# Records of the edges scattered straight from their tiles, 224 in the dense layers' block and 168 behind the experts' stores

## The chip, the cores and the metric

The kernel runs on one core of a Trainium2 chip. A core has the engines PE (TensorE, matrix products), VectorE (DVE), ScalarE (ACT), GpSimd (POOL) and SyncE (SP), which here only issues DMAs. Each engine runs its own stream of instructions, in order, and they meet at semaphores. The metric is device time in microseconds of one execution, the median of several runs.

## What is computed

A graph of 3125 nodes with 256 channels and 50000 edges (src, dst), sorted by dst, passes two layers, each a graph part and a feed-forward part, with a layer norm ahead of each part and a residual sum behind it:

```python
edge_index = jnp.stack([src, dst])
x = x + _L0_gnn_ref(_layernorm(x), edge_index, ...)   # sum of x[src] at dst, then 256-512-1024-512-256 with batch norm and elu
x = x + _L0_ffn_ref(_layernorm(x)[None], ...)[0]      # 8 experts, top 2 of a router, silu(x w1) * (x w3), then w2
x = x + _L1_gnn_ref(_layernorm(x), ..., edge_index)   # attention over edges: e = exp(leaky(el[src] + er[dst])), sums at src
x = x + _L1_ffn_ref(_layernorm(x)[None], ...)[0]      # the half of the nodes with the largest weights goes through gelu(x w1) w2
```

The second graph part sums at src, while the edges come sorted by dst. So the kernel sorts them anew, by the block of 125 nodes that src lies in, and this sorting is what the change touches.

## The kernel before

The program is a row of blocks. At the end of each block all engines meet at a barrier. In order, with the times of the profiled execution:

- 0 to 546 us, edges of the first layer: GpSimd gathers 128 rows at a time of the normalised x (L312, 392 indirect DMAs), PE sums them by one-hot matrices, VectorE adds the sums. Beside it VectorE ranks each edge within its source block.
- 546 to 1065 us, the dense layers (four matmul layers with batch norm). VectorE first turns the ranks into places, tile `posd` (L714, ready at 587.9 us). Then GpSimd scatters the records.
- 1065 to 1224 us, the router of the experts: layer norm, logits, top 2, places of the rows in tiles of 128 by expert; GpSimd scatters the normalised rows to `xs_d` (L976, 50 indirect DMAs), and the experts' weights are split in two f16 halves.
- 1224 to 1624 us, the experts: 56 tiles of 128 rows, in one block with the router. For each tile PE makes `psH` and `psY`, ScalarE writes `yv`, and GpSimd stores `yv` to `y_d` (L983).
- 1624 to 1720 us the results are gathered and added and the table of the second graph part is written; 1720 to 2326 us the edges of the second layer; 2326 us to the end its feed-forward part.

A record is 8 bytes for an edge: its place in its source block and its dst. Tile `rec` (128 partitions x 392 columns x 2) holds them, tile `posd` (128 x 392) the place of each in the DRAM tensor `rec_d`. Both lie untouched in SBUF until the second layer's edges, where `rec_d` is loaded. One indirect DMA scatters one column, 128 records, so 392 of them are needed (T1 = 392). They are made in 49 rounds (R1) of 8 columns, each round in two halves of four (HT = 4). `stage` (L590 to L600) makes a half: two copies on GpSimd bring the four columns of `posd` to `stp` (L592) and of `rec` to `str_` (L593), a wait on `s_stg` lets them finish, and four indirect DMAs (L597) read the small tiles. Since the small tiles have two halves, each half waits on `s_sc[h]` until the scatters of the half before it in the same place have landed.

LATE = 12 sets where they stand. In the dense layers' block GpSimd makes the first 37 rounds, 296 scatters: two halves in straight code, then a hardware loop (L627). The other 12 rounds, 96 scatters, stand in the experts' block, in a loop in which each store of a tile is followed by one half (L985); in a second loop the other 32 stores follow without scatters (L990). At the end of the block GpSimd waits until all scatters and stores have landed. GpSimd does nothing else in the dense block but one memset. All of this is written in program order; no scheduler moves it.

SyncE loads in the dense block, behind the third layer's matmuls, x again (`x2`), the bias `b4` and the raw weights of four of the eight experts (L565, L570), those of the others at the start of the router's block.

Of the kernel before, what the change touches and what calls it, by code (L numbers as in the profile page):

```python
# [31 lines left out]
I32 = mybir.dt.int32  # L32
# [12 lines left out]
TPR = 8  # L45
HT = TPR // 2
R1 = -(-E // (ET * TPR))
T1 = R1 * TPR
# [10 lines left out]
T2 = (K2 * N + X * 127) // 128  # L59
# [16 lines left out]
def wait_apart(eng, sem, value, tick):  # L76


    eng.wait_ge(sem, value)
    eng.sem_inc(tick, 1)  # L80


def loop(nc, eng, start, end):

    return nc.Fori(start, end, engines=[eng.engine], hint_back_edge=True)
# [25 lines left out]
def program(nc, a, out):  # L111
    with ExitStack() as ctx:
        taken = []

        def sem(name):
            taken.append(nc.alloc_semaphore(name))
            return taken[-1]
# [10 lines left out]
        KB = 1024  # L128
        BASE = 16512

        def at(name, offset, shape, dt=F32):
            return nc.alloc_sbuf_tensor_at(name, shape, dt, offset=BASE + offset)

        def dram(name, shape, dt=F32):
            return nc.dram_tensor(name, shape, dt, kind="Internal").ap()

        xn_d = dram("xn_d", (N, D))
        rec_d = dram("rec_d", (ET, T3 * 2), I32)
# [4 lines left out]
        rec = at("rec", 1 * KB, [128, T1, 2], I32)  # L143
# [94 lines left out]
        s_halves = sem("s_halves")  # L238
# [277 lines left out]
        behind = at("behind", 101 * KB, [T3 // HT, HT, NB])  # L516
        blk_i = at("blk_i", 101 * KB + 512, [T3 // HT, HT], I32)
        posd = at("posd", 1 * KB + 3136, [128, T1], I32)
        stp = at("stp", 1 * KB + 4704, [128, 2, HT], I32)
        str_ = at("str_", 1 * KB + 4736, [128, 2, HT, 2], I32)  # L520
        LATE = 12
        blk_d = dram("blk_d", (1, T3), I32)
        zero = at("zero", 153 * KB, [128, D])
        xs_d = dram("xs_d", (T2 * 128, D))
# [6 lines left out]
        s_pos = sem("s_pos")  # L531
        s_blk = sem("s_blk")
        s_blkst = sem("s_blkst")
        s_stg = sem("s_stg")
        s_sc = [sem("s_sc0"), sem("s_sc1")]
        s_sq = sem("s_sq")
        s_sd = sem("s_sd")
# [41 lines left out]
        with ExitStack() as p2:  # L579
# [7 lines left out]
                f = ZIN[l][:, k, :].bitcast(F16)  # L587
                return f[:, bass.ds(c0 * 2, w)], f[:, bass.ds(c0 * 2 + w, w)]

            def stage(pool, g, h):  # L590

                nc.gpsimd.tensor_copy(stp[:, h, :], posd[:, bass.ds(g * TPR + h * HT, HT)])  # L592
                nc.gpsimd.tensor_copy(str_[:, h, :, :], rec[:, bass.ds(g * TPR + h * HT, HT), :]).then_inc(s_stg, 1)  # L593
                pool.wait_ge(s_stg, g * 2 + h + 1)
                pool.sem_inc(s_halves, 1)
                for j in range(HT):
                    pool.indirect_dma_start(  # L597
                        out=rec_d.rearrange("p (t r) -> (p t) r", r=2),
                        out_offset=bass.IndirectOffsetOnAxis(ap=stp[:, h, j:j + 1], axis=0),
                        in_=str_[:, h, j, :], in_offset=None).then_inc(s_sc[h], 16)  # L600

            @block.sync
            def _(sp):
# [14 lines left out]
            @block.gpsimd  # L618
            def _(pool):
                ch = Chain(pool, s_c2[0])  # L620
                nc.gpsimd.memset(zero[:, :], 0.0).then_inc(s_zero, 1)

                pool.wait_ge(s_recst, 16)
                pool.wait_ge(s_pos, 1)
                stage(pool, 0, 0)
                stage(pool, 0, 1)
                with loop(nc, pool, 1, R1 - LATE) as g:  # L627
                    for h in range(2):
                        pool.wait_ge(s_sc[h], g * (16 * HT))
                        stage(pool, g, h)  # L630

            def rows_of(l, m):

# [258 lines left out]
        yv = at("yv", o, [128, 2, D]); o += 2048  # L892
        y_d = dram("y_d", (T2 * 128, D))
# [29 lines left out]
        s_yv = sem("s_yv")  # L923
        s_yst = [sem("s_yst0"), sem("s_yst1")]

        with ExitStack() as p3:
# [36 lines left out]
            @block.gpsimd  # L963
            def _(pool):
                ch = Chain(pool, s_c3[0])
                nc.gpsimd.memset(ones3[:, :], 1.0)
                ch.step(nc.gpsimd.memset(later3[:, :], 1.0))
                ch.step(nc.gpsimd.affine_select(out=later3[:, :], in_=later3[:, :], compare_op=ALU.is_gt, fill=0.0,
                                                base=0, pattern=[[1, PB]], channel_multiplier=-1))
                pool.sem_inc(s_k3, 1)  # L970

                pool.wait_ge(s_slot, 1)
                for b in range(NB):
                    for k in range(K2):
                        j = b * K2 + k
                        pool.indirect_dma_start(  # L976
                            out=xs_d, out_offset=bass.IndirectOffsetOnAxis(ap=slot_i[:, j:j + 1], axis=0),
                            in_=xn2[:, b, :], in_offset=None).then_inc(s_scx, 16)


                def store(t, i):
                    wait_apart(pool, s_yv, 1 + t + 1, s_halves)
                    pool.dma_start(y_d[bass.ds(t * 128, 128), :], yv[:, i, :]).then_inc(s_yst[i], 16)  # L983

                with loop(nc, pool, 0, LATE) as g:  # L985
                    for i in range(2):
                        store(g * 2 + i, i)
                        pool.wait_ge(s_sc[i], (g + (R1 - LATE)) * (16 * HT))
                        stage(pool, g + (R1 - LATE), i)
                with loop(nc, pool, LATE, T2 // 2) as g:  # L990
                    for i in range(2):
                        store(g * 2 + i, i)
                for h in range(2):
                    pool.wait_ge(s_sc[h], 16 * HT * R1)
                for i in range(2):
                    pool.wait_ge(s_yst[i], 16 * (T2 // 2))

# [930 lines left out]
```

## Time and profile before

| | us |
|---|---|
| three runs | 2622.04, 2623.48 (median), 2626.05 |
| the profiled execution, its own time | 2622.28 |
| its span | 2620.7 |
| GpSimd busy | 1480.6 (56%) |
| PE busy | 1861.2 (71%) |
| VectorE busy | 1496.4 (57%) |
| ScalarE busy | 631.6 (24%) |

The profile gives for each engine the times at which it executed. "Idle before" an instruction is time in which the engine had nothing running, with the releaser that ended it; "issue" is time in which it waited for nothing that the profile shows, and a releaser such as PEq L579 is the sequencer of another engine at a barrier. Since blocks are closed by barriers, the engine that ends a block last sets its length, and idle time of the others there costs nothing.

### The profile page before, as it was taken

The page shows a single profiled execution, that of the slowest core. Times are in us where ns is not written, and L with a number is a line of the kernel's source. Part 1 is how long each engine was busy: PE and PEld are TensorE (multiplying, and loading weights), DVE is VectorE, ACT ScalarE, POOL GpSimd, SP SyncE. Part 2 cuts the span into 40 slices and gives each one's busy share as a digit, 9 for nine tenths or more (in the row PEclk, how much of TensorE's full clock was granted, in tenths as well). Part 3 has the DMA queues.
Part 4 walks back from the last instruction along what each step waited for, and adds up shares of the span by engine and source line. Part 5 has one row for each costly group of instructions (what it writes and reads, how often), then busy time and mean ns, then how long its engine had stood idle before and what let it go on. Part 6 is the DMA issues. An engine that isn't in the chain of part 4 may idle for free. (4 is left out here: it accounts for less than half of the span.)

```text
span 2620.7 us, 37949 instructions
## 1 busy us (share of the span) xinstructions
PE 1861.2 (71%) x9564; PEld 1336.1 (51%) x9565; DVE 1496.4 (57%) x3214; ACT 631.6 (24%) x1252; POOL 1480.6 (56%) x1583
## 2 busy tenths in 40 slices
PE   3988889898979650405999996267788777731597
PEld 2766667743434340403666664256566656620366
DVE  7666544465567370471333333646666666668698
ACT  4000000025566340151333332121111111110343
POOL 3777777717777777174662002757777777751000
PEclk8555665588989875557999998568887888865699
DMA  7333333340000230321111111321111111120100
GB/s 219 106 102 104 104 105 104 105 139 1 1 1 1 74 113 1 128 72 55 37 37 37 39 36 41 89 59 25 26 25 25 25 25 25 25 12 0 25 24 26
DMA packets 112944, 144.01 MB, mean 55 GB/s; under 512 B 46660, under 2 KB 82372, under 8 KB 112764
## 3 DMA queue, kind: packets, MB, share of 16 engines
q0 software_dynamic: 60160, 86.81, 13.8%
q1 hardware_dynamic: 52729, 56.58, 7.0%
q8 instruction: 20, 0.33, 0.0%
q14 instruction: 35, 0.29, 0.0%
HBM read 114.00 MB, written 29.18 MB: 55 GB/s over the span
## 5 line engine op out<-in xcount | busy, mean ns | idle before, releaser
L1484 POOL DMA_INDIRECT g<-tab_d,recs x416 | 460.0, 1106 | 148.8 <-issue 126.5
L597 POOL DMA_INDIRECT rec_d<-str__1722,stp x392 | 393.2, 1003 | 172.5 <-issue 94.6
L497 PE MATMUL psA<-oh,G 128*128 128x128 f32 x1568 | 433.4, 438 | 73.6 <-DMA G<-xn_d,gat_i 35.7
L312 POOL DMA_INDIRECT G<-xn_d,gat_i x392 | 378.6, 966 | 145.0 <-issue 134.3
L497 PEld LDWEIGHTS psA<-oh,G 128*128 128x128 f32 x1568 | 340.4, 303 | 166.6 <-issue 93.2
L1625 PE MATMUL psS<-vv,oh 128*125 128x260 f32 x832 | 307.9, 523 | 128.6 <-DVE acc L1560 128.6
L1625 PEld LDWEIGHTS psS<-vv,oh 128*125 128x125 f32 x832 | 180.4, 245 | 222.1 <-DVE acc L1560 183.1
L825 PE MATMUL psZ<-z,W 128*128 (+1 forms) x1344 | 264.0, 359 | 27.0 <-DVE z L739 27.0
L447 DVE TENSOR_TENSOR accT<-accT,psA 128x256 f32 x392 | 165.0, 421 | 167.6 <-PE psA L497 141.6
L643 ACT ACTIVATE z<-psZ,vec 128x500 f32 (+2 forms) x112 | 70.8, 633 | 640.7 <-PE psZ L818 530.9
L1234 PE MATMUL psH<-we,xh 128*128 x1344 | 214.7, 310 | 0.5 <-issue 0.5
L825 PEld LDWEIGHTS psZ<-z,W 128*128 128x128 f16 x1344 | 124.5, 98 | 166.4 <-issue 39.3
L1560 DVE TENSOR_TENSOR acc<-acc,psS 125x260 f32 x416 | 176.6, 424 | 43.6 <-PE psS L1625 2.4
L983 POOL DMA_DIRECT2D y_d<-yv x56 | 31.3, 558 | 237.6 <-ACT yv L1041 236.9
L1234 PEld LDWEIGHTS psH<-we,xh 128*128 128x128 f16 x1344 | 130.6, 98 | 60.6 <-issue 8.1
L1493 ACT ACTIVATE ohT<-psOT 125x512 f32<-125x512 f32 x104 | 62.1, 597 | 379.6 <-PE psOT L1609 379.6
L1549 DVE TENSOR_TENSOR vv<-g,pp 128x1040 f32<-128x1040 f32 x104 | 128.6, 1236 | 23.1 <-PE psS L1625 17.0
L1617 PEld LDWEIGHTS psE<-el,ohT 125*128 125x128 f32 x832 | 130.5, 224 | 13.2 <-issue 2.4
L1150 DVE SCALAR_TENSOR_TENSOR hv<-psH,sl 128x384 f32<-128x384 f32 x112 | 57.5, 513 | 129.6 <-ACT sl L1029 129.6
L1144 DVE SCALAR_TENSOR_TENSOR xh<-psTx,xh 128x256 f16<-128x256 f32 x56 | 23.8, 424 | 182.8 <-ACT xh L1023 182.8
L1255 PE MATMUL psY<-we,hh 128*128 (+1 forms) x1008 | 125.3, 273 | 1.1 <-DVE hh L1157 1.1
L1617 PE MATMUL psE<-el,ohT 125*128 x832 | 116.1, 263 | 1.8 <-ACT ohT L1493 1.8
(253 smaller groups left out, 2728.4 us busy)
## 6 DMA issues: line engine op xcount, KB each, us to landing
raw<-in_L_ffn_w SPq DMA_DIRECT2D x16, 682.0 KB, 9.3
xs_d<-zero SPq DMA_DIRECT2D x1, 7168.0 KB, 23.9
xs<-xs_d SPq DMA_DIRECT2D x56, 128.0 KB, 2.0
y_d<-yv POOLq DMA_DIRECT2D x56, 128.0 KB, 2.0
g<-tab_d,recs POOLq DMA_INDIRECT x416, 2.5
G<-xn_d,gat_i POOLq DMA_INDIRECT x392, 2.7
rec_d<-str__1722,stp POOLq DMA_INDIRECT x392
raw<-in_L_ffn_w SPq DMA_DIRECT2D x16, 384.0 KB, 9.8
```

Source lines behind the costliest of these rows:

```text
L312: pool.indirect_dma_start(out=G[:, i, :], out_offset=None, in_=xn_d, in_offset=bass.IndirectOffsetOnAxis(ap=gat_i[:, t:t + 1], axis=0)).th ...
L447: nc.vector.tensor_tensor(accT[:, :, bass.ds(at_[i], WIN)], accT[:, :, bass.ds(at_[i], WIN)], psA[i // 2][:, i % 2, :, :], ALU.add).then_i ...
L497: last = nc.tensor.matmul(psA[i // 2][:, i % 2, h, :], G[:, i, 128 * h:128 * (h + 1)], oh[:, i, :], start=True, stop=True)
L597: pool.indirect_dma_start(out=rec_d.rearrange("p (t r) -> (p t) r", r=2), out_offset=bass.IndirectOffsetOnAxis(ap=stp[:, h, j:j + 1], axis=0),
L825: last = nc.tensor.matmul(psZ[m % 4][:, 0:w], W[l][:, sw, k, ms], halves(l, k, c * CW, w)[sh], start=(n == 0), stop=(n == len(terms) - 1))
L1234: last = nc.tensor.matmul(psH[2 * w3 + q][:, 0:HC[q]], xh[:, i, sx, 128 * k:128 * (k + 1)], weights(e, 2 * w3 + k, sw, q * HQ, HC[q]), sta ...
L1255: last = nc.tensor.matmul(psY[:, :], hh[0:KP[m], i, sh, 128 * m:128 * (m + 1)], weights(e, 4 + n, sw, (m - 3 * n) * D, D)[0:KP[m], :], sta ...
L1484: pool.indirect_dma_start(out=g3[:, n % BODY, j, :], out_offset=None, in_=tab_d, in_offset=bass.IndirectOffsetOnAxis(ap=recs[:, t, 1:2], a ...
L1549: nc.vector.tensor_tensor(vv[:, s % 2, :, :].rearrange("p j (h f) -> p j h f", h=NH), g3[:, s, :, NH:RW].unsqueeze(2).to_broadcast([128, H ...
L1560: nc.vector.tensor_tensor(b, b, psS[j][:, :], ALU.add).then_inc(s_ac, 1)
L1617: last = nc.tensor.matmul(psE[s % 2][:, j, :], ohT[:, s % 2, 128 * j:128 * (j + 1)], el[:, bass.ds(at_[j] * NH, NH)], start=True, stop=True)
L1625: last = nc.tensor.matmul(psS[j][:, :], oh3[:, s, j, :], vv[:, s % 2, j, :], start=True, stop=True)
```

## The change

The staging is taken out. `record(pool, t)` issues one indirect DMA that reads its 128 places from column t of `posd` and its records from column t of `rec`; the tiles `stp` and `str_`, the semaphore `s_stg` and the waits for landed halves go. The split between the blocks is now by columns: EDGES_EARLY = 224 in the dense layers' block, and behind each of the 56 stores of the experts PER_TILE = 3, 168 in all. Both are straight code in place of hardware loops, and the store addresses are constants. The waits at the end of the experts' block remain.

```diff
-        stp = at("stp", 1 * KB + 4704, [128, 2, HT], I32)
-        str_ = at("str_", 1 * KB + 4736, [128, 2, HT, 2], I32)
-        LATE = 12
+        EDGES_EARLY = 224
+        PER_TILE = (T1 - EDGES_EARLY) // T2
+        assert EDGES_EARLY + PER_TILE * T2 == T1
...
-            def stage(pool, g, h):
-
-                nc.gpsimd.tensor_copy(stp[:, h, :], posd[:, bass.ds(g * TPR + h * HT, HT)])
-                nc.gpsimd.tensor_copy(str_[:, h, :, :], rec[:, bass.ds(g * TPR + h * HT, HT), :]).then_inc(s_stg, 1)
-                pool.wait_ge(s_stg, g * 2 + h + 1)
-                pool.sem_inc(s_halves, 1)
-                for j in range(HT):
-                    pool.indirect_dma_start(
-                        out=rec_d.rearrange("p (t r) -> (p t) r", r=2),
-                        out_offset=bass.IndirectOffsetOnAxis(ap=stp[:, h, j:j + 1], axis=0),
-                        in_=str_[:, h, j, :], in_offset=None).then_inc(s_sc[h], 16)
+            def record(pool, t):
+                pool.indirect_dma_start(
+                    out=rec_d.rearrange("p (t r) -> (p t) r", r=2),
+                    out_offset=bass.IndirectOffsetOnAxis(ap=posd[:, t:t + 1], axis=0),
+                    in_=rec[:, t, :], in_offset=None).then_inc(s_sc[t % 2], 16)
...
                 pool.wait_ge(s_recst, 16)
                 pool.wait_ge(s_pos, 1)
-                stage(pool, 0, 0)
-                stage(pool, 0, 1)
-                with loop(nc, pool, 1, R1 - LATE) as g:
-                    for h in range(2):
-                        pool.wait_ge(s_sc[h], g * (16 * HT))
-                        stage(pool, g, h)
+                for t in range(EDGES_EARLY):
+                    record(pool, t)
...
                 def store(t, i):
-                    wait_apart(pool, s_yv, 1 + t + 1, s_halves)
-                    pool.dma_start(y_d[bass.ds(t * 128, 128), :], yv[:, i, :]).then_inc(s_yst[i], 16)
-
-                with loop(nc, pool, 0, LATE) as g:
-                    for i in range(2):
-                        store(g * 2 + i, i)
-                        pool.wait_ge(s_sc[i], (g + (R1 - LATE)) * (16 * HT))
-                        stage(pool, g + (R1 - LATE), i)
-                with loop(nc, pool, LATE, T2 // 2) as g:
-                    for i in range(2):
-                        store(g * 2 + i, i)
-                for h in range(2):
-                    pool.wait_ge(s_sc[h], 16 * HT * R1)
+                    pool.wait_ge(s_yv, 1 + t + 1)
+                    pool.dma_start(y_d[t * 128:(t + 1) * 128, :], yv[:, i, :]).then_inc(s_yst[i], 16)
+
+                for t in range(T2):
+                    store(t, t % 2)
+                    for j in range(PER_TILE):
+                        record(pool, EDGES_EARLY + t * PER_TILE + j)
+                for i in range(2):
+                    pool.wait_ge(s_sc[i], 16 * (T1 // 2))
                 for i in range(2):
                     pool.wait_ge(s_yst[i], 16 * (T2 // 2))
```

What stands in a row on GpSimd in the dense layers' block before; the copies fill the small tiles, each DMA row is four scatters, and the second part is the body of a hardware loop of 36 rounds:

```order
L621 MEMSET zero 128x256
L592 COPY stp<-posd 128x4
L593 COPY str__1722<-rec 128x8
L597 DMA rec_d<-str__1722,stp 53248x2 x4
L592 COPY stp<-posd 128x4
L593 COPY str__1722<-rec 128x8
L597 DMA rec_d<-str__1722,stp 53248x2 x4
L627 UNCONDITIONAL_BRANCH
```

The same place now, and what follows it up to the rows' scatters of the router's block (L965, was L976):

```order
L614 MEMSET zero 128x256
L590 DMA rec_d<-rec,posd 53248x2 x224
L578 UNCONDITIONAL_BRANCH
L952 UNCONDITIONAL_BRANCH
L955 MEMSET ones_4989 128x125
L956 MEMSET later_4988 128x125
L957 AFFINE_SELECT later_4988<-later_4988 128x125
L965 DMA xs_d<-xn_4987,choice 7168x256 x50
```

The 224 scatters now stand in one row with no copy, wait or branch between them.

GpSimd among the experts before, one store and one half round of the loop body (the ISA rows are register work):

```order
L983 DMA y_d<-yv 128x256
L988 ISA
L592 ISA
L592 COPY stp<-posd 128x4
L593 ISA
L593 COPY str__1722<-rec 128x8
L594 ISA
L597 DMA rec_d<-str__1722,stp 53248x2 x4
```

The same place now, the first three tiles of 56:

```order
L972 DMA y_d<-yv 128x256
L590 DMA rec_d<-rec,posd 53248x2 x3
L972 DMA y_d<-yv 128x256
L590 DMA rec_d<-rec,posd 53248x2 x3
L972 DMA y_d<-yv 128x256
L590 DMA rec_d<-rec,posd 53248x2 x3
```

Each store is followed by three scatters, in all 56 tiles and so behind the last store too, where before the last 32 stores had none behind them. The streams of PE, VectorE, ScalarE and SyncE keep their instructions.

## Rows read from the trace of the kernel before

**Rows 1.** The page's 40 slices of 65.5 us: busy tenths of PE and GpSimd.

```profile
PE   3988889898979650405999996267788777731597
...
POOL 3777777717777777174662002757777777751000
```

**Rows 2.** Stretches: from:to, length, busy us and instructions by engine, clock, DMA share, GB/s.

```profile
975.00:1059.00 84.00, 0.00 (x0) 0.00 (x0) 0.00 (x0) 0.00 (x0) 59.72 (x86) 0.51 0.02 1
979.00:983.00 4.00, 0.00 (x0) 0.00 (x0) 0.00 (x0) 0.00 (x0) 3.19 (x5) 0.50 0.02 1
1119.00:1210.00 91.00, 0.07 (x1) 0.10 (x2) 43.55 (x52) 37.93 (x48) 67.89 (x50) 0.50 0.29 79
1224.00:1396.00 172.00, 159.66 (x1198) 112.81 (x1199) 57.12 (x120) 58.44 (x144) 113.52 (x167) 1.00 0.13 37
1410.00:1582.00 172.00, 159.66 (x1198) 112.58 (x1196) 57.02 (x120) 58.47 (x144) 12.95 (x24) 1.00 0.11 37
```

**Rows 3.** Timeline rows at three barriers: start us, length, instruction, [idle before].

```profile
544.05 0.57 DVE L467 COPY pos<-psT 128x392 f32<-128x392 f32 x1
...
545.75 0.31 POOL L621 MEMSET zero<- 128x256 f32 x1 [6.38 <-POOLq L243]
...
974.19 0.42 DVE L746 SCALAR_TENSOR_TENSOR x<-psO,x 125x256 f32<-125x256 f32 x1 [0.62 <-PE psO L842]
...
1065.17 1.73 DVE L1072 BATCH_NORM_STATS2 bst<-x 125x6 f32<-125x256 f32 x5 [90.56 <-PEq L579]
...
1065.14 0.20 POOL L966 MEMSET ones<- 128x125 f32 x1 [6.18 <-POOLq L579]
...
2324.28 2.13 DVE L1560 TENSOR_TENSOR acc<-acc,psS 125x260 f32 x4 [2.39 <-PE psS L1625]
...
2326.69 0.20 POOL L1731 MEMSET earlier<- 125x125 f32 x1 [16.17 <-POOLq L1470]
```

**Rows 4.** Timeline, GpSimd: the first scatter, and the first ones of two half rounds.

```profile
589.07 1.03 POOL L597 DMA_INDIRECT rec_d<-str__1722,stp  x1 [0.85 <-POOL str__1722 L593]
...
1048.31 0.98 POOL L597 DMA_INDIRECT rec_d<-str__1722,stp  x1 [0.79 <-POOL str__1722 L593]
...
1054.19 0.98 POOL L597 DMA_INDIRECT rec_d<-str__1722,stp  x1 [0.79 <-POOL str__1722 L593]
```

**Rows 5.** Groups by line, 587 to 975 us: busy us, mean ns, idle before.

```profile
L597 POOL DMA_INDIRECT rec_d<-str__1722,stp x239 | 245.4, 1027 | 105.9 <-issue 57.7 <-POOL str__1722 L593 47.6 <-DMA rec_d<-str__1722,stp 0.6
...
L734 DVE TENSOR_SCALAR z<-yb 128x500 f32 (+2 forms) x112 | 40.4, 393 | 3.2 <-DVE yb L731 3.1
```

**Rows 6.** Groups by line, GpSimd, whole span.

```profile
L312 POOL DMA_INDIRECT G<-xn_d,gat_i x392 | 378.6, 966 | 145.0 <-issue 134.3 <-PE psA L497 10.7
...
L976 POOL DMA_INDIRECT xs_d<-xn,choice x50 | 67.9, 1358 | 71.4 <-DVE choice L1130 53.2 <-issue 18.3
```

**Rows 7.** Timeline at 917 us, GpSimd and VectorE.

```profile
917.90 6.37 POOL L592 COPY stp<-posd 128x4 int32 x1 [1.07 <-DMA rec_d<-str__1722,stp]
...
917.39 6.82 DVE L782 TENSOR_TENSOR x<-x,b 125x6400 f32<-125x6400 f32 x1
```

**Rows 8.** Timeline, GpSimd: the first and the last two stores of the experts, and what follows.

```profile
1225.21 0.63 POOL L983 DMA_DIRECT2D y_d<-yv  x1 [20.03 <-ACT yv L1041]
...
1612.26 0.54 POOL L983 DMA_DIRECT2D y_d<-yv  x1 [6.41 <-ACT yv L1041]
1616.40 0.54 POOL L983 DMA_DIRECT2D y_d<-yv  x1 [3.61 <-ACT yv L1041]
1624.21 0.14 POOL L1390 MEMSET row<- 125x25 f32 x1 [7.26 <-POOLq L122]
```

**Rows 9.** DMA issues: tensors, queue, count, KB each, median us to landing.

```profile
y_d<-yv POOLq DMA_DIRECT2D x56, 128.0 KB, 2.0
g<-tab_d,recs POOLq DMA_INDIRECT x416, 2.5
...
xs_d<-xn,choice POOLq DMA_INDIRECT x50, 3.9
```

More of the change, by code:

```diff
@@ L533, in program @@
         s_blkst = sem("s_blkst")
-        s_stg = sem("s_stg")
         s_sc = [sem("s_sc0"), sem("s_sc1")]
```

## Prediction

> **What bounds the kernel now.** I read the page's busy times and slices first [rows 1]. The kernel is a row of blocks, each closed by a barrier of all engines, so its span is a sum of stages, and the question for each stage is which engine arrives last. In the sixteenth slice (983 to 1048 us) PE stands at 0 and GpSimd at 7 tenths. The table by stretches puts numbers to it: from 975 to 1059 us PE, VectorE and ScalarE have no instruction, GpSimd 86: one engine works alone [rows 2]. The ends and starts at the barrier say the same: VectorE's last instruction of the dense layers ends at 974.19 + 0.42 = 974.61, and its next stood idle for 90.56 us; GpSimd's next begins at 1065.14 after 6.18 us, so its last scatter ended at 1058.96 [rows 3]. So the dense block ends with GpSimd, 84.3 us after VectorE, and then has a tail of 6.18 us.
>
> From 588 to 1059 GpSimd runs 37 rounds of two half rounds. One half round: two copies, 0.79 us of idling between the second copy and the first scatter, four scatters with 0.30 us between them, 5.88 us in all in the quiet stretch (1048.31 to 1054.19) [rows 4]. That is 1.47 us a scatter, of which 0.96 is the scatter, 0.30 its issue and the rest the staging.
>
> Among the experts it is PE that bounds: stretches of 172 us with 95 of the scatters and with none have the same 1198 PE instructions and the same 159.66 us of PE, and in the first of them GpSimd is busy 113.52 us of 172 [rows 2].
>
> **Dense layers, number of scatters and price of one.** 296 scatters become 224, 72 fewer, and the 74 pairs of copies go. After the change a scatter is the indirect DMA alone with its issue. Bounds: the gathers of L312 are the same form (offsets read from a column of a large tile, no copy between, 392 in straight code) at 966 ns each, + 0.30 = 1.27 us; the scatters of L597 beside busy VectorE, 587 to 975 us, are at 245.4 / 239 = 1.027 us, + 0.30 = 1.33 us [rows 5, 6]. I take 1.33, as the 224 lie in that same stretch. GpSimd then starts at about 588.9 (the posd it waits for is ready where it was, and the first scatter now starts no later than 589.07 [rows 4]) and ends at 588.9 + 224 x 1.33 = 886.8, plus the tail of 6.18: 893. By 1.27 it is 879.6. VectorE ends at 974.61 as before: GpSimd is early by 82 us. It would be last again only if a scatter cost over (974.61 - 6.18 - 588.9) / 224 = 1.70 us.
>
> **What is late next.** VectorE at 974.61. Of SP's loads none is under way after 975: the DMA engines are 0.02 busy there, and 1 GB/s is the scatters' own [rows 2]. PE and ScalarE show no instruction after 975 either. The tail after an engine that isn't GpSimd: at the end of the edges' block GpSimd had been idle for 16.17 us, VectorE ended at 2324.28 + 2.13 = 2326.41, and the next block began at 2326.69, 0.28 us later. At the end of the first block it took 1.13 us after VectorE (544.05 + 0.57 = 544.62 to 545.75), but there GpSimd's own tail, 6.38 us from 539.37, may have set it [rows 3]. I take 0.28 and keep 1.13. New start of the router's block: 974.89 (975.74). Gain 1065.14 - 974.89 = **90.25 us** (89.40).
>
> **Does the start of the router's block change?** PE will have idled some 4 us before its first transposes instead of 90, so one could hope for a higher clock. But the granted clock was already at 0.50, the 1.2 GHz level, in 979 to 983, when PE had been idle for 5 us [rows 2], and ahead of the first transposes stand VectorE's statistics of five blocks, 1.73 us [rows 3], and their normalising, which brings PE's start to about that moment. I take 0.
>
> **Copies removed.** They read and write SBUF beside VectorE. Once a copy stood 6.37 us, while VectorE added b4 to all of x2 for 6.82 us [rows 7]. GpSimd lost there; VectorE didn't. In the experts' two stretches VectorE's busy time is 57.12 us beside the copies and 57.02 without [rows 2], so for VectorE I take 0, with -1 us as the other end.
>
> **Waits removed.** The copy of rows 7 also shows GpSimd waiting for landed scatters, 1.07 us, and there is no other limit on scatters in flight afterwards. They don't pile up: with the scatters alone on the chip the 16 DMA engines are 0.02 busy [rows 2]. The nearest row for unpaced scatters is L976, 50 of them, 18.3 us of idle on issue, 0.37 each instead of 0.30 [rows 6]: by it 224 cost 16 us more, and GpSimd still ends before 910. Hidden by VectorE's 974.61; without that cover it would be 16 us.
>
> **Experts, three scatters behind each of 56 stores.** 168 instead of 96 there. A tile costs GpSimd 0.54 + 0.30 + 3 x 1.26 = 4.6 us, against 391.2 / 55 = 7.11 us from store to store (first 1225.21, last 1616.40) [rows 8]. With four scatters and two copies it was more, and PE lost nothing by it. So no store goes later than now and PE waits for nothing: 0, up to tile 54.
>
> **End of the experts.** Here the new scatters are not covered. Before, the last store ran 1616.40 to 1616.94 and the next block began at 1624.21 on GpSimd [rows 8]. After: store 54 at 1612.26 to 1612.80, three scatters to 1612.80 + 3 x 1.26 = 1616.6, store 55 to 1617.15, three scatters to 1617.15 + 3.78 = 1620.93, then the wait for their landing. That is 3.99 us later. A store lands in 2.0 us; for the scatters no landing is shown, the nearest are the gathers g at 2.5 and the row scatters xs_d at 3.9 [rows 9]. I take 2.6: 3.99 + 0.6 = **4.6 us**. Low end 4.0, if landing changes nothing; high end 8.2, if a tail of 6.2 us, as after the scatters of the dense block, comes on top in place of the 2.0.
>
> **Sum.** Against the profiled execution, span 2620.7 and time 2622.28: 2622.28 - 90.25 + 4.6 = 2536.6. The median of the runs, 2623.48, is 1.2 above it: **2537.8**, some 3.3% faster.
>
> **Rivals.** (a) GpSimd still arrives last at the end of the dense layers, since a scatter straight from rec and posd is dearer than one from the small tiles. At the mean of L976, 1.358 + 0.37 = 1.73 us, it would end at 588.9 + 387.5 + 6.2 = 982.6, and the kernel at 2545.5; at 1.80 us, 2561. For it: beside VectorE the scatters of L597 are already 0.07 us dearer than in the quiet. Against: the mean of 239 of them, and L312 [rows 5, 6].
>
> (b) The same dearness taken further makes the kernel **slower**. With c the price of a scatter, the loss in the dense block is 224c - 380 and among the experts, from c = 2.1 on, 56 x (3c + 0.9) - 403. At c = 2.08 the first alone eats the 86 us; at c = 2.5 the sum is 180 + 68 - 86 = +162, or 2786. A mechanism would be that VectorE and the writing of a scatter's descriptors shut each other out. But if each of the 112 tensor_scalars of L734 in the stretch held up GpSimd for its whole length, that would be 40.4 us [rows 5], and 893 + 40 = 933 is still ahead of 974.61. The rows show no mean of an indirect DMA above 1.36.
>
> By the Trainium skill (SBUF — State Buffer, "SBUF: two separate sides") a DMA issued from GpSimd starves while VectorE runs a two-port operation, since its descriptors can't be written; it has one of about 0.62 us taking 3.1 us (an estimate by that page's figure for all 224: the dense block would end at 1289 and the kernel near 2850). This trace doesn't agree with it as the common case: the scatters beside VectorE took 1.03 us in the mean. I give that outcome 0.01, inside (b).
>
> (c) The clock of the experts. PE loses 84 us of idling before them. If the chip then granted it the lower level, the 160 us of PE in a stretch of 24 tiles, 373 us in 56, would cost up to 373 more [rows 2], and from 23% of them on the gain is gone (2911 at worst). For it: nothing but that PE is granted 0.50 elsewhere. Against: 91 us of idle PE (1119 to 1210) still stand ahead of the experts [rows 2].
>
> (d) No change: the barrier waited for something else until 1065. Against: no other engine shows an instruction after 975.
>
> **How the numbers follow.** Forecast 0.88; (a) 0.05; (b) 0.02; (c) 0.02; (d) 0.02; the rest, 0.01, slower. Range: the forecast's terms reach from 2536 (experts' end 4.0, copies -1) to 2542 (tail 1.13, experts' end 8.2). Single executions differ by 4 us (2622.04 to 2626.05), which gives 2532 to 2546; to take in (a) at its nearer price I put the top at 2550, and the low end at 2531. A difference of 0.2%, 5 us, is about what can be told from none: faster 0.93, same 0.02, slower 0.05.
>
> **What would show it.** In the changed kernel's trace: 224 scatters at 1.26 to 1.35 us from start to start, ending near 887; VectorE's idle before the router's block under 2 us by the barrier's name; no stretch of 84 us with GpSimd alone; the experts' tiles at 7.1 us; the last expert instruction on PE to the next block some 4.6 us longer than before. I am wrong if scatters cost over 1.70 us, or if the router's block starts later than 976.

## The result, and the profile after

Four runs of the changed kernel took 2530.33 to 2536.93 us, median 2534.78; four runs of the kernel before on the same chip took 2622.04 to 2626.28, median 2624.77. The ratio is 0.9656, 95% interval 0.9639 to 0.9673: 3.4% faster, 3.0 us under the forecast of 2537.8 and inside the range. The profiled execution took 2535.8 us, its span is 2534.1.

The timeline of the changed kernel at the end of the dense layers (start us, length, instruction, idle before in brackets), first GpSimd, then VectorE:

```profile
883.92 0.97 POOL L590 DMA_INDIRECT rec_d<-rec,posd  x1 [0.30 <-issue]
973.27 0.20 POOL L955 MEMSET ones<- 128x125 f32 x1 [88.37 <-POOLq L578]
...
972.56 0.42 DVE L735 SCALAR_TENSOR_TENSOR x<-psO,x 125x256 f32<-125x256 f32 x1 [0.62 <-PE psO L831]
```

These answer to [rows 3]. GpSimd's last early scatter ends at 884.89 instead of 1058.96, and GpSimd is now the one that idles, 88.37 us. VectorE ends at 972.98 and the next block begins 0.29 us later, at 973.27; before it began at 1065.14.

GpSimd's group of scatters in 587 to 975 us (busy us, mean ns, idle before), which answers to [rows 5]:

```profile
L590 POOL DMA_INDIRECT rec_d<-rec,posd x224 | 227.3, 1015 | 111.2 <-issue 69.4 <-DVE posd L703 41.8
```

And three stretches (from:to, length, busy us with instructions of PE, PE's weight loads, VectorE, ScalarE, GpSimd; clock, DMA share, GB/s), which answer to [rows 2]:

```profile
975.00:1059.00 84.00, 32.44 (x158) 31.48 (x158) 65.02 (x228) 38.21 (x66) 26.65 (x18) 0.52 0.40 130
1132.00:1304.00 172.00, 159.70 (x1199) 112.82 (x1198) 57.12 (x120) 58.03 (x144) 84.21 (x96) 1.00 0.12 37
1318.00:1490.00 172.00, 159.67 (x1199) 112.72 (x1197) 57.12 (x120) 58.53 (x144) 84.14 (x96) 1.00 0.12 37
```

The 84 us in which GpSimd worked alone hold the router's block now. Among the experts PE does its 1199 instructions in the same 159.7 us, with 96 stores and scatters on GpSimd (24 tiles of one store and three scatters) in place of 167 instructions.

The end of the experts on GpSimd, which answers to [rows 8]:

```profile
1523.59 0.58 POOL L972 DMA_DIRECT2D y_d<-yv  x1
1524.47 0.99 POOL L590 DMA_INDIRECT rec_d<-rec,posd  x1 [0.30 <-issue]
1527.04 0.96 POOL L590 DMA_INDIRECT rec_d<-rec,posd  x1 [1.58 <-issue]
1528.30 0.97 POOL L590 DMA_INDIRECT rec_d<-rec,posd  x1 [0.30 <-issue]
1533.05 0.14 POOL L1375 MEMSET row<- 125x25 f32 x1 [3.77 <-POOLq L122]
```

From the start of the last store to the next block it is 9.46 us, where it was 1624.21 - 1616.40 = 7.81: 1.65 us more.

The sum by stages, before against after: start of the router's block 1065.14 to 973.27, that is -91.87; from there to the first store 160.07 to 158.85, -1.22; from first to last store 391.19 to 391.47, +0.28; end of the experts +1.65; the rest of the kernel, 996.49 to 1001.05, +4.56. Together -86.6, the difference of the spans. The +4.56 lies in code that the change doesn't touch.

### The profile page after: what moved, and what is told of

Its sections match the earlier page's. It is cut to its first block and busy times, and to the rows that moved or that the text cites. A ratio compares the mean times of both kernels' runs of the same rounds, so it can differ in the third digit from the quotient of the medians.

```text
span 2534.1 us, 36898 instructions
## 1 busy us (share of the span) xinstructions
PE 1855.5 (73%) x9564; PEld 1333.1 (53%) x9565; DVE 1496.6 (59%) x3214; ACT 632.3 (25%) x1252; POOL 1435.1 (57%) x1387
## 5 line engine op out<-in xcount | busy, mean ns | idle before, releaser
L590 POOL DMA_INDIRECT rec_d<-rec,posd x392 | 391.4, 999 | 166.3 <-issue 124.5
L497 PE MATMUL psA<-oh,G 128*128 128x128 f32 x1568 | 428.2, 434 | 78.4 <-DMA G<-xn_d,gat_i 39.6
L1129 DVE SCALAR_TENSOR_TENSOR xh<-psTx,xh 128x256 f16<-128x256 f32 x56 | 23.8, 424 | 182.7 <-ACT xh L1008 182.7
## 6 DMA issues: line engine op xcount, KB each, us to landing
xs_d<-zero SPq DMA_DIRECT2D x1, 7168.0 KB, 23.8
```

The costliest lines, as they stand in the source:

```text
L497: last = nc.tensor.matmul(psA[i // 2][:, i % 2, h, :], G[:, i, 128 * h:128 * (h + 1)], oh[:, i, :], start=True, stop=True)
L590: pool.indirect_dma_start(out=rec_d.rearrange("p (t r) -> (p t) r", r=2), out_offset=bass.IndirectOffsetOnAxis(ap=posd[:, t:t + 1], axis=0 ...
```

## Experiments

Two sorts of chip came up. On the chip of the result and on that of e0, f1, f2 and e5 (whether it is another one isn't on record) the kernel before takes 2625 us, and the first block of the kernels traced there ends at 543 to 549 us. On two others it takes 2799 us (e1 to e4) and 2832 us (e1b, e4b, g1, e0b); there the first block ends at 630 to 640 us, and the page's slices show 84 to 90 GB/s in it against 101 to 106. Each kernel is compared with the kernel before on its own chip. I call these the first and the second sort. The runs of a chip were taken together, so whether the sort belongs to the chip or to the state that it was in isn't shown. In three theories of what follows, S is GpSimd's long straight code, W its unbroken row of scatters without waits, P the program's own placement.

The lower GB/s don't come from gathers that are issued more slowly. GpSimd's waits in the first block, 100 to 500 us, where the code of all kernels is the same, in the changed kernel on the first sort (the result's profile) and then on the second (e0b; us in total, times, longest):

```profile
POOL G L312 <- PE psA L497: 5.2, 17, 0.3
```

```profile
POOL G L312 <- PE psA L497: 77.7, 38, 3.4
```

On the second sort GpSimd stands still until TensorE has used the rows gathered before; in between its gathers go out 1.25 us apart as on the first, TensorE's own waits for gathered rows add up to 34.2 us against 31.9, and one store of 7168 KB by SyncE lands in 23.8 us in both profiles. TensorE waits 50.3 us for VectorE's one-hot matrices, where on the first sort no such wait is among the large ones. So the second sort is slower between the engines beside GpSimd already in the first block, ahead of the code that the change touches; why stays open.

**e1: the split alone.** The copies, waits and loops stay; only the number of rounds among the experts changes, so that 224 scatters are early and 168 late.

```
-        LATE = 12
+        LATE = 21
```

> The kernel before with its staging, copies, waits and hardware loops as they are, and LATE = 21 in place of 12: 28 rounds (224 scatters) in the dense layers' block, 21 rounds (168) behind the first 42 stores of the experts. Theory 1 (the gain is the number of scatters ahead of the barrier, and the staging costs nothing once GpSimd isn't last): GpSimd makes its 28 rounds at (1058.96 - 588) / 37 = 12.73 us each, ends at 944 and with its tail at 951, ahead of VectorE at 973 to 975, so the router's block starts at 973.3 to 974.9 and the whole gain of that block is there, 90 us; the experts' tiles stay at 7.11 us, and no scatter stands behind the last 14 stores: span some 2530 to 2534, 89 to 91 us under the kernel before. Theory 2 (the cheaper scatters carry the gain): without them less than half of it is there, 2575 or more. Side question: if it is GpSimd's copies that cost VectorE 1.6 us in the dense layers, VectorE ends at 974 to 975 here; if it is the scatters that stood beside the last layer, at about 973.

Measured, second sort: 2729.12 us, ratio 0.9759 (0.9702 to 0.9817). **e1b** is the same kernel on the other chip of that sort.

> The same kernel as e1: the kernel before with 224 scatters early and 168 late, staged by copies and in its loops. f1, the same as straight code, took 2532 us against the changed kernel's 2532. If leaving a hardware loop costs nothing (e5 showed its 6.2 us tail behind straight code too): 2531 to 2534 us where the kernel before takes 2624, ratio 0.965. If the straight code is what made f1's dense layers end 2 to 4 us earlier after the block's start: about 2535 us, 0.966.

Measured: 2786.38 us, ratio 0.9857 (0.9814 to 0.9899). A gain is there with every copy in place, 70 and 46 us; both intervals lie below 1, though e1b's gain is under 2%. VectorE ends the dense layers in both (GpSimd's last early scatter at 1031.8 and 1031.6, VectorE at 1075.9 and 1117.0). It takes 445.5 and 479.7 us from the block's first memset to VectorE's end, where the same split takes 428.1 on the first sort (f1, below): the staged form is slowed there too. The expectation of e1b for a chip where the kernel before takes 2624 us stayed untested.

**e2, e3, e4: no copies, other splits.** Each is the changed kernel with another pair of numbers: 296 early and two behind each of the first 48 stores; 336 early and one behind each store; 224 early and four behind each of the first 42 stores. e4, the others alike:

```
-        EDGES_EARLY = 224
-        PER_TILE = (T1 - EDGES_EARLY) // T2
+        EDGES_EARLY, PER_TILE, TILES = 224, 4, 42
...
-                    for j in range(PER_TILE):
+                    for j in range(PER_TILE if t < TILES else 0):
```

> The changed kernel with the split of before: 296 scatters straight from posd and rec in the dense layers' block, 2 behind each of the first 48 stores. GpSimd ends at 588.2 + 296 x 1.32 = 979, some 6 us after VectorE (973), so it ends the block again. Theory 1: the next block starts when GpSimd is through, at 979 plus its tail. If the tail of 6.18 us belongs to any indirect DMA, that is 985; if it belongs to leaving a hardware loop, as there is none here, it is 981. So the staging's removal alone gives 80 to 84 us of the 90 in that block: span 2532 to 2541. Theory 2 differs little here; a price of a scatter above 1.36 us would show as an end after 991.

> The changed kernel with 336 scatters in the dense layers' block and 1 behind each store of the experts. GpSimd is last for certain: 588.2 + 224 x 1.33 to 886, then 112 more at 1.27 to 1.33, ending at 1029 to 1035, 56 to 62 us after VectorE. Loop-exit theory: the next block starts 0.3 to 2.5 us after GpSimd's last scatter. Drain theory: 6.2 us after it. Span by the first: about 2534.1 + 58 + 1 - 3 = 2590, by the second 2595. It also prices a scatter at the margin: 40 more than in e2 should cost 40 x 1.27 = 51 us.

> The changed kernel with 224 scatters early and 4 behind each of the first 42 stores, none behind the last 14 (168 in all). A tile costs GpSimd 0.57 + 0.3 + 4 x 1.27 = 6.0 us, under the 6.5 to 7.9 between stores, so the tiles stay at 7.11 us. After the last yv of ScalarE: by the loop-exit theory the next block starts 8.56 - 3.6 = 5 us later, 5 us sooner than in the changed kernel (10.03), since the store ends some 1.3 us after yv, lands 2.0 later and the barrier takes 1.7; by the theory that the end of this block costs what it cost before whatever GpSimd does, 8.6 us later, 1.5 us sooner. Span 2529 or 2533, with noise of 3 us around either, so the trace decides.

Measured, second sort: e2 3058.04 us, ratio 1.0941 (1.0886 to 1.0996); e3 3109.87 us in one run, 1.111; e4 2960.23 us, 1.0576 (1.0524 to 1.0628). No theory of mine had any of these. GpSimd had ended early enough (e4: last early scatter at 964 us, VectorE at 1321). It was TensorE that crawled, in the second of the dense layers. So the three say nothing on the price of the copies, for which they were meant, and the crawl became the question.

**e4b: the same as e4; e0b: the changed kernel itself, both on a chip of the second sort.**

> The same kernel as e4 (224 scatters beside the dense layers, 4 behind each of the first 42 stores of the experts, none behind the last 14). It asks whether TensorE's crawl belongs to this program or to the chip it ran on. Theory C (the chip on which the first block ends 88 us later): where the kernel before takes about 2624 us, no crawl, 96 TensorE instructions in 20 us beside the scatters, and, with no scatter behind the last store, the experts' end some 3.9 us shorter than the changed kernel's (f1 has 5.6 us from the last store to the next block, the changed kernel 9.5): ratio 0.963 to 0.966, about 2528 us. Theory P (this program, wherever it runs): the crawl, ratio 1.05 to 1.06. Where the kernel before takes about 2799 us, both expect the crawl.

> The changed kernel once more, so that it stands beside e4 on the same chip. Where the kernel before takes about 2624 us: 2532 (0.965), no crawl. Where it takes about 2799: theory C expects the crawl here too, from some 80 us after the layers' start beside the scatters until some 17 us behind the last, and a ratio of 1.03 to 1.06; theory P expects none and 0.966 to 0.970.

Measured: e4b 3018.44 us, 1.0671 (1.0623 to 1.0720); e0b 3002.37 us, 1.0607 (1.0581 to 1.0632). The changed kernel, 3.4% faster on the first sort, is 6% slower here. Stretches of e0b, columns as above:

```profile
740.00:780.00 40.00, 8.62 (x15) 1.57 (x15) 0.68 (x1) 0.68 (x1) 30.52 (x32) 0.50 0.02 1
900.00:940.00 40.00, 7.86 (x14) 1.45 (x14) 3.14 (x5) 2.74 (x4) 30.68 (x31) 0.50 0.02 1
1020.00:1060.00 40.00, 40.00 (x191) 18.34 (x189) 23.99 (x40) 21.52 (x32) 0.00 (x0) 1.00 0.00 0
```

And the same two places in e1b, on the same chip, with the scatters staged in a loop:

```profile
740.00:780.00 40.00, 40.00 (x191) 18.32 (x189) 23.89 (x40) 21.89 (x32) 29.43 (x38) 1.00 0.02 1
900.00:940.00 40.00, 40.00 (x191) 18.33 (x190) 29.48 (x54) 27.14 (x40) 29.75 (x38) 1.00 0.02 1
```

Beside the unstaged scatters TensorE does 14 or 15 matmuls in 40 us at a granted clock of 0.50, the 1.2 GHz level; beside the staged ones 191 at 1.00. VectorE and ScalarE wait for it. The clock isn't the cause: at the lower level a matmul is 0.58 us, and between two of them TensorE stands idle for 2.2 us. Its timeline in e0b, just before the crawl ends:

```profile
966.99 0.58 PE L814 MATMUL psZ<-z,W 128*128 x1 [2.22 <-issue]
969.79 0.58 PE L814 MATMUL psZ<-z,W 128*128 x1 [2.22 <-issue]
...
990.79 1.30 PE L814 MATMUL psZ<-z,W 128*128 x2 [2.21 <-issue]
992.88 1.28 PE L814 MATMUL psZ<-z,W 128*128 x2 [0.80 <-issue]
994.32 0.58 PE L814 MATMUL psZ<-z,W 128*128 x1 [0.15 <-issue]
995.70 4.75 PE L814 MATMUL psZ<-z,W 128*128 x11 [0.81 <-issue]
```

From start to start it is a multiple of about 0.7 us, in most cases 2.8 or 2.1, at most 4.9, and all idle time is "issue": the profile shows nothing that TensorE waits for. The crawl begins at 711.6 us, 31 us after the first scatter, some 50 matmuls into the second layer, and ends at about 995, 26 us behind the last early scatter (969.3). It is there in all six runs of unstaged kernels on the second sort (e2, e3, e4, e4b, e0b, g1), and in e2 and e3 it is longer with the row of scatters: their last ends at 1063 and 1120, the crawl at about 1090 and 1142. Between e0b and e1b it costs 1329.83 - 1116.98 = 212.9 us at VectorE's last instruction of the dense layers (1.2 of them stood there before the block began). Theory P, that the crawl belongs to some programs by where their instructions lie, wherever they run, falls: the same program crawls on the second sort (e0b) and not on the first (e0, below).

**e0: the changed kernel again; f1: staged, but in straight code; f2: unstaged, with the old waits.** These were to divide S from W; they met a chip of the first sort.

f1 is e1 with the early loop written out:

```
-                with loop(nc, pool, 1, R1 - LATE) as g:
+                for g in range(1, R1 - LATE):
```

f2 is the changed kernel with the waits back (and the two semaphores taken in turn by fours):

```
                 for t in range(EDGES_EARLY):
+                    if t % HT == 0 and t >= 2 * HT:
+                        pool.wait_ge(s_sc[t // HT % 2], 16 * HT * (t // HT // 2))
                     record(pool, t)
```

> The changed kernel itself, on whatever chip this call gets. Question: three kernels that share its 224 unstaged scatters beside the dense layers (4, or 2, or 1 behind a store later) showed, on a chip whose first block ended 88 us later than in the blind profile, a stretch from some 80 us after the layers' start of the unstaged scatters to some 17 us after the last of them, in which TensorE did 7 to 8 instructions in 20 us in place of 96. Theory W (unstaged scatters in an unbroken row, with no wait between them, do this to TensorE on a chip where transfers are slow): if the kernel before takes about 2799 us here, this kernel has the crawl too and stands at 1.05 of it (about 2950); if the kernel before takes about 2624, it stands at 0.966 and 96 instructions in 20 us stay. Rival P (the crawl belongs to those three programs, by where their instructions lie): no crawl and 0.966 to 0.970 on either sort of chip.

> 224 scatters beside the dense layers with copies and waits as before, but written out as straight code in place of the loop (168 beside the experts, in the loop). Theory S (GpSimd's stream of instructions out of no loop takes from TensorE what TensorE's own instructions come by): on a chip with the crawl this kernel has it too, 7 to 8 TensorE instructions in 20 us while the scatters run, and ratio 1.03 to 1.06. Theory W (it is the unbroken row of scatters without waits): no crawl, ratio 0.976 as the same kernel with the loop. On a chip without the crawl both expect 0.974 to 0.977. Of the end of the dense layers: if the 6.2 us tail of GpSimd in the kernel before is the leaving of a loop, it is 3 to 4 us here; if it is the landing of scatters, 6.2 us stay.

> The changed kernel with the copies gone but with the old waits: ahead of each four scatters of the first 224, GpSimd waits until the four of two groups before have landed. Theory W: no crawl on any chip, and the time is that of the changed kernel on a chip without the crawl, or up to 0.4% above it (56 groups, each waiting at most the 2.1 us landing less the 4 x 1.0 us of the group between, so mostly nothing). Theory S: on a chip with the crawl it has it as well, ratio 1.04 to 1.06.

Measured, against 2624.61: e0 2531.91 us, 0.9651 (0.9635 to 0.9667); f1 2532.12 us, 0.9648 (0.9632 to 0.9664); f2 2534.56 us, 0.9657 (0.9639 to 0.9675). No crawl in any. The stretch 760 to 800 us of e0, f1 and f2, in this order, one row of each:

```profile
760.00:800.00 40.00, 40.00 (x188) 18.14 (x186) 31.08 (x57) 27.93 (x42) 30.85 (x31) 0.98 0.02 1
```

```profile
760.00:800.00 40.00, 40.00 (x191) 18.31 (x190) 30.97 (x57) 27.07 (x40) 28.25 (x37) 1.00 0.02 1
```

```profile
760.00:800.00 40.00, 40.00 (x185) 18.00 (x184) 30.10 (x55) 27.26 (x40) 31.16 (x30) 0.97 0.02 1
```

The three are one time within their intervals, so **on this sort, once the split is moved, neither the copies nor the waits are worth anything**: the split alone gives the whole gain. It doesn't follow that dropping the copies would have given nothing by itself. At the 1.325 us that an unstaged scatter took, 296 of them would end at 588.19 + 392.1 = 980.3 and the block at 986.5 with the tail of 6.18, 79 us earlier than before (an estimate). The kernel that asks this, e2, ran on the second sort only. The reason is in f1's rows at the end of the dense layers:

```profile
947.78 1.19 POOL L597 DMA_INDIRECT rec_d<-str__1722,stp  x1 [0.30 <-issue]
970.95 0.20 POOL L966 MEMSET ones<- 128x125 f32 x1 [21.99 <-POOLq L579]
```

With copies and waits the 224 scatters end at 948.97, 64 us later than in the changed kernel, and still 22 us ahead of the barrier that VectorE sets. Among the experts it is the same: PE does 1199 instructions in 159.65 us in f1's 172 us with 168 instructions on GpSimd. f1 expected 3 to 4 us in place of the 6.2 us tail; GpSimd was not last, so it shows no tail. Where S and W differ nothing was told, since both expect no crawl here.

**e5: the last two early rounds behind the loop.** The kernel before, in straight code for its last 16 early scatters.

```
-                with loop(nc, pool, 1, R1 - LATE) as g:
+                with loop(nc, pool, 1, R1 - LATE - 2) as g:
...
+                for g in range(R1 - LATE - 2, R1 - LATE):
+                    for h in range(2):
+                        pool.wait_ge(s_sc[h], g * (16 * HT))
+                        stage(pool, g, h)
```

> The kernel before, with its early rounds' last two (16 scatters of the 296, their copies and waits) written out behind the loop; every instruction is the same. It asks what the 6.2 us between GpSimd's last scatter beside the dense layers and the next block are. Theory L (leaving the loop, with code behind it that has to come first): the pause moves to the loop's new end, two rounds earlier, and is partly hidden or not, and behind the last scatter 3 to 4 us stay: the block starts 0 to 3 us earlier, ratio 0.999 to 1.000. Rival D (the last scatters' landing and the draining of the queue): 6.2 us stay behind the last scatter, no pause at the loop's end, ratio 1.000.

Measured: 2620.56 us, ratio 0.9986 (0.9973 to 0.9999), 4 us that I can't place. Its rows:

```profile
1061.27 0.96 POOL L597 DMA_INDIRECT rec_d<-str__1722,stp  x1 [0.30 <-issue]
1068.41 0.20 POOL L970 MEMSET ones<- 128x125 f32 x1 [6.18 <-POOLq L579]
```

The tail is 6.18 us to the hundredth as in [rows 3], behind straight code, and at the loop's new end there is no pause (scatters go on 1.26 to 1.29 us apart in a half and 2.06 to 2.08 from half to half, as before it). Theory L, that leaving the loop costs it, falls. That it is the scatters' landing and the queue's draining fits, but isn't shown.

**g1: x in two loads.** With VectorE the bound, its longest wait in the changed kernel's dense layers, 18.0 us, is the one for the bias b4 and x. g1 is e4 with the load cut in two, and the bias ahead of it:

```
-                sp.dma_start(x2[:, :, :], a["x"].rearrange("(b p) d -> p b d", p=PB)).then_inc(s_xr, 16)
                 sp.dma_start(b4[:, :], a["L0_gnn_b4"].partition_broadcast(PB)).then_inc(s_b4, 16)
+                xv = a["x"].rearrange("(b p) d -> p b d", p=PB)
+                sp.dma_start(x2[0:112, :, :], xv[0:112]).then_inc(s_xr, 16)
+                sp.dma_start(x2[112:PB, :, :], xv[112:PB]).then_inc(s_xr, 16)
```

and VectorE's wait raised to 32.

> A version meant to be better: e4 with the load of x beside the last dense layer in two pieces, of 112 and of 13 partitions, and with the bias load ahead of it. In the changed kernel VectorE waits 18.0 us for them (to 917.2) and the load moves 121 GB/s, with the expert weights behind it 370 GB/s. Theory R (125 partitions spread over few of the 16 DMA engines; 112 spread over all): x lands before VectorE comes to it at 899.2, the wait is gone, the dense layers end 16 to 18 us earlier, and the next block with them; the expert weights start earlier as well: 2510 to 2514 us, ratio 0.957. Rival Q (the rate is that of 1 KB pieces from x's rows, whatever their spread): the load lands where it did, the gain is 0 to 1 us, ratio 0.964.

Measured, second sort: 3005.65 us, ratio 1.0623 (1.0602 to 1.0644), against e4b's 1.0671 (1.0623 to 1.0720) on the same chip, 12.8 us between the medians. The loading stretch of e4b, then that of g1:

```profile
1248.00:1264.00 16.00, 8.17 (x48) 7.35 (x48) 6.39 (x12) 8.55 (x12) 0.00 (x0) 0.59 0.34 121
```

```profile
1248.00:1257.00 9.00, 1.53 (x6) 1.04 (x6) 4.88 (x10) 7.25 (x10) 0.00 (x0) 0.52 1.09 241
1260.00:1268.00 8.00, 4.88 (x35) 4.64 (x33) 0.00 (x0) 0.23 (x1) 0.00 (x0) 0.87 1.07 144
```

And VectorE's wait, e4b and then g1:

```profile
1275.44 0.42 DVE L768 SCALAR_TENSOR_TENSOR b<-psR,b 125x256 f32<-125x256 f32 x1 [17.85 <-DMA b<-in_L_gnn_b]
```

```profile
1258.43 0.42 DVE L770 SCALAR_TENSOR_TENSOR b<-psR,b 125x256 f32<-125x256 f32 x1
1269.99 6.83 DVE L772 TENSOR_TENSOR x<-x,b 125x6400 f32<-125x6400 f32 x1 [11.14 <-DMA x<-in_x]
```

Theory R is half right. In pieces the DMA engines are busy throughout (share 1.09 against 0.34) and the load moves 241 GB/s instead of 121, but then it shares them with the experts' weights behind it (144 GB/s at 1260) and lands 11 us late instead of 18. The block of the router starts 1333.16 - 1325.59 = 7.6 us earlier, of the 16 to 18 expected. The bias no longer waits behind x, but VectorE needs x right after it, so the 6.7 us less of waiting are the pieces' doing.

## Why the prediction was right, point by point

- *GpSimd ends the dense block last.* Right; f1 shows that the split alone lifts it.
- *224 scatters at 1.33 us, ending at 886.8.* (884.89 - 588.19) / 224 = 1.325 us, ending at 884.89.
- *VectorE is late next, at 974.61, and the barrier follows 0.28 us later.* It ended at 972.98, and the barrier took 0.29 us, so the 0.28 and not the 1.13. The gain was 91.87 instead of 90.25. Counted from the memset that begins the block, VectorE ends after 428.86 (before), 428.89 (e5) and 428.08 us (f1) beside the copies, and after 426.90 (changed), 427.60 (e0) and 426.37 us (f2) without. The two groups don't overlap and lie 0.5 to 2.5 us apart, which fits the -1 us that I had given the copies as the other end; with three executions each it isn't shown.
- *Waits removed: hidden.* f2 puts them back: GpSimd ends at 882.73, the ratio is the same. The 18.3 us rate of [rows 6] didn't come.
- *No change at the router's start.* The first store comes 158.85 us after the block's start instead of 160.07. I had 0; 1.2 us was left out.
- *The experts' tiles at 7.11 us.* 391.47 / 55 = 7.12.
- *End of the experts +4.6.* This is the mis-sized term: it measured +1.65, below the low end of 4.0. The scatters themselves took more than I had: the last ended 5.68 us after the start of the last store where my numbers give 4.3, with a pause of 1.58 us ahead of the second (1.57 in e0) that I can't explain. The miss is in the tail. I had let the store's whole tail of 7.26 us [rows 8] stand behind the last scatter, as a landing of 2.0 and a fixed rest. Behind the last scatter it is 3.77 us (3.77 in e0, 4.10 in f2), the landing of 2.1 us (the page's median for rec_d in the changed kernel) within it, so the 7.26 was no fixed price. In f1, with copies, loops and no scatter behind the last stores, it is 5.07 (e1b 5.06), in e4, unstaged and straight with none there either, 4.77. What makes it 7.26, 5.07 or 3.77 stays open; e5 excludes the loop only for the other tail.
- *Everything after is as before.* It was 4.56 us longer in this profile. In e0, the same kernel, that part is 2528.8 - 1533.77 = 995.0 us, in f1 1003.7, in f2 1000.3, though its code is the same. Why it differs by up to 9 us isn't shown. In the profiled execution it covered the errors of the terms above, which had the other sign (-1.6 in the dense layers, -1.2 at the router's start, -2.9 at the experts' end). A sum this close to the time is partly luck.
- *Rival (a), (b) and the skill's starving.* The scatter beside VectorE took 1.015 us in the mean, 1.47 at most by its line in the trace. By the Trainium skill (SBUF — State Buffer, "SBUF: two separate sides") a DMA starved by VectorE takes 3.1 us; no scatter here did. On the second sort a scatter from start to start is (969.31 - 680.95) / 224 = 1.29 us.
- *Rivals (c) and (d).* The clock in the experts' stretches is 1.00 as before, and the barrier came with VectorE, so neither held.
- *The chance of slower.* The mechanism that makes this change slower was none of my rivals: not GpSimd's price, but TensorE's supply beside it, and only on another sort of chip. I had taken TensorE's pace beside the scatters as given because the trace of before shows it so; that trace held staged scatters in a loop, on one chip. I didn't ask what replacing the loop by hundreds of instructions in a row could do to another engine.

**Left open: the cause of the crawl.** Shown: it came with the second sort of chip and the changed form of the scatters together; the staged loop on the same chip has no such crawl. Not separated: S (straight code) from W (no waits), and either from the missing copies, since f1 and f2 ran on the first sort alone. The experts of the same runs say that straight code alone doesn't bring it. Stretches of e0b and then of e1b, each from its first store:

```profile
1490.00:1662.00 172.00, 159.72 (x1198) 112.69 (x1197) 57.78 (x120) 58.69 (x143) 84.10 (x96) 1.00 0.12 37
```

```profile
1276.00:1448.00 172.00, 155.59 (x1138) 106.30 (x1135) 53.97 (x115) 53.12 (x137) 106.28 (x158) 1.00 0.12 36
```

In e0b GpSimd's code among the experts is straight too, with a wait for `yv` after every three scatters, and TensorE does its 1198 instructions as on the first sort. (In e2, with two scatters behind a store, it does 1199.) With the staged scatters of e1b it does 1138: from first to last store it is 409 us against e0b's 392 (391 on the first sort), and with four scatters behind a store (e4b) 413. So there the changed form is the faster one, and what the second sort holds up depends on how densely GpSimd works as well as on the form; that this is the cause is argued, not shown.

One view speaks for the supply of TensorE's instructions. In e1b the chunk of 125 columns behind TensorE's loop, code that runs once, came in small groups while staged scatters ran, from 824.3 to 848.2 us:

```profile
827.26 0.79 PE L825 MATMUL psZ<-z,W 128*128 128x125 f16 x6 [0.44 <-issue]
828.71 0.58 PE L825 MATMUL psZ<-z,W 128*128 128x125 f16 x4 [0.66 <-issue]
830.15 0.58 PE L825 MATMUL psZ<-z,W 128*128 128x125 f16 x4 [0.87 <-issue]
```

In e0b, where that chunk ran 100 us after the last scatter, it has no gap (nor has it in f1 beside staged scatters, on the first sort):

```profile
1073.79 19.50 PE L814 MATMUL psZ<-z,W 128*128 x162
```

The groups of e1b begin about 0.7 or 1.4 us apart, steps that the crawl has too. That the supply of instructions is the cause is argued, not shown; and the crawl's last 26 us, with no scatter left, fit no theory well. The runs that would separate S from W are f1 and f2 on a chip of the second sort.

## What to carry to other kernels

When a barrier has one late engine, first move its work to where another engine is the bound; only then ask whether that work can be made cheaper. Here moving 72 scatters gave the whole gain on one sort of chip, where making them cheaper as well added nothing, and on the other the form that made them cheaper went with a loss of 6% where the staged form gained. A kernel that writes hundreds of DMA issues out in a row should be timed on more than one chip: the safer form here is e1's, 0.976 and 0.986 on the two chips where the changed form is 1.058 (e4) and 1.061 (e0b), though e1 itself wasn't measured on the first sort (f1, its straight twin, has 0.965 there). And the engine that becomes the bound should be read at once for its own longest wait; here 18 us stood in a load of 125 partitions.

## What was not expected of the hardware

- One kernel, two sorts of chip: 2625 against 2799 and 2832 us, with 104 against 88 GB/s in the gathers of the first block. GpSimd waits there for TensorE for 77.7 us of 400 against 5.2, and issues its gathers as fast between.
- TensorE at one matmul in 2.8 us, with nothing shown that it waits for, beside GpSimd's unstaged scatters on the second sort.
- A load of 125 partitions in pieces of 1 KB moved 121 GB/s at a DMA share of 0.34; 112 and 13 partitions moved 241 at 1.09.
- The tail of 6.18 us at a block's end behind GpSimd's scatters is the same out of a loop and out of straight code; that behind the last scatter of the experts was 3.77 to 4.10.
